# Two transformer layers with routed experts: the token table without weights, its one-hots on VectorE, output additions on GpSimd

## What is computed

```python
# layer 0: 8 experts of width 256, top 2, softmax router, shared width 1024
x = x + tanh(g_ffn[0]) * ffn0(layernorm(x))
# layer 1: 32 experts of width 192, top 6, sigmoid router, shared width 384
x = x + tanh(g_ffn[1]) * ffn1(layernorm(x))

def ffn(x):                                  # both, in outline
    topk_w, topk_i = top_k(score(x @ gate_w), K)
    topk_w = topk_w / sum(topk_w)
    combine = one_hot(topk_i) weighted by topk_w       # tokens x experts
    routed = einsum(silu(x @ wg[e]) * (x @ wu[e]) @ wd[e], combine)
    shared = silu(x @ sg) * (x @ su) @ sd
    return routed + shared
```

## Time and profile before

| | |
|---|---|
| runs | 2045.34 us median of 3 (2045.24 to 2046.21) |
| profiled execution | 2046.07 us, its span 2044.0 us |
| mean granted clock of TensorE | 0.969 |
| busy TensorE | 1886.2 us (92% of the span) |
| busy VectorE | 1348.0 us (66%) |
| busy ScalarE | 1145.5 us (56%) |
| busy GpSimd | 782.2 us (38%) |

### The profile page before, as it was taken

How to read it: one execution, slowest core, us unless ns; L and a number is a source line. 1 busy time by engine, 2 the same in 40 slices (tenths; PEclk the granted TensorE clock), 3 DMA queues, 4 the chain that set the end, 5 groups by cost and what they waited for, 6 DMA issues and landing times. The chain is left out here.

```text
span 2044.0 us, 40829 instructions
## 1 busy us (share of the span) xinstructions
PE 1886.2 (92%) x10024; PEld 1220.2 (60%) x10025; DVE 1348.0 (66%) x2556; ACT 1145.5 (56%) x1857; POOL 782.2 (38%) x941
## 2 busy tenths in 40 slices
PE   5999999989999999994999999987888999999998
PEld 2333333344888878872433333345667888888886
DVE  6899988841445544436889988859984555555553
ACT  1777777753322335541777777762224566666664
POOL 3222222125201125553222222127644656565555
PEclk9999999999999999995999999988999999999998
DMA  4422222142111458665422222131027888888886
GB/s 141 119 59 64 61 66 64 40 172 97 55 55 56 144 175 196 139 107 138 123 67 59 65 60 67 45 136 39 1 96 180 190 196 203 194 201 201 204 186 107
DMA packets 100082, 233.53 MB, mean 114 GB/s; under 512 B 17410, under 2 KB 20484, under 8 KB 99972
## 3 DMA queue, kind: packets, MB, share of 16 engines
q1 hardware_dynamic: 61572, 137.75, 23.7%
q0 software_dynamic: 33792, 79.71, 20.1%
q10 hardware_dynamic: 4608, 14.68, 2.2%
HBM read 127.23 MB, written 57.67 MB: 90 GB/s over the span
## 5 line engine op out<-in xcount | busy, mean ns | idle before, releaser
L599 DVE TENSOR_REDUCE maxima<-ring_ps 128x1 f32<-128x512 f32 x1024 | 639.8, 681 | 89.2 <-PE ring_ps L386 88.2
L493 ACT ACTIVATE probs<-score_ps 128x1024 f32<-128x1024 f32 x512 | 501.8, 1019 | 91.6 <-PE score_ps L403 89.3
L386 PE MATMUL ring_ps<-k_turned,q_turned 64*128 64x512 f32 x1024 | 414.3, 481 | 39.7 <-DMA q_turned<-q_lo 18.4
L386 PEld LDWEIGHTS ring_ps<-k_turned,q_turned 64*128 64x128 f32 x1024 | 179.0, 193 | 367.1 <-DVE maxima L599 258.0
L1179 PE MATMUL bank_f<-w_gu_parts_f,xg_T_f 128*128 x1800 | 367.1, 352 | 2.1 <-issue 2.1
L1179 PEld LDWEIGHTS bank_f<-w_gu_parts_f,xg_T_f 128*128 128x128 f32 x1800 | 325.8, 190 | 30.4 <-issue 3.0
L403 PE MATMUL score_ps<-q_turned,k_turned 64*128 64x512 f32 x1024 | 336.3, 447 | 1.7 <-ACT probs L493 1.4
L420 PE MATMUL out_ps<-probs,v_ones 128*32 128x512 f32 x2048 | 273.3, 606 | 10.7 <-issue 10.4
L1204 PE MATMUL bank_f<-w_dn_parts_f,hg_T_f 96*128 (+1 forms) x888 | 243.6, 410 | 1.5 <-DVE hg_T_f L1773 1.5
L983 POOL DMA_INDIRECT xg_f<-xh_rows_f,idx_in_f x156 | 159.5, 1022 | 186.1 <-DVE idx_in_f L1663 106.7
L999 POOL DMA_INDIRECT out_x<-y_tok_f,idx_out_f x111 | 177.2, 1596 | 133.0 <-ACT y_tok_f L1407 94.6
(11 more groups left out here) (232 smaller groups left out, 2335.2 us busy)
## 6 DMA issues: line engine op xcount, KB each, us to landing
w_gu_f<-in_L_w_gu SPq DMA_DIRECT2D x64, 384.0 KB
q_turned<-q_hi SPq DMA_DIRECT2D x128, 128.0 KB, 2.6
w_raw_f<-in_L_w_sh_gu ACTq DMA_DIRECT2D x28, 512.0 KB, 3.5
w_dn_f<-in_L_w_dn SPq DMA_DIRECT2D x32, 384.0 KB
k_turned<-k_hi SPq DMA_DIRECT2D x128, 64.0 KB, 2.1
q_turned<-no_max SPq DMA_DIRECT2D x64, 128.0 KB, 2.6
q_turned<-q_lo SPq DMA_DIRECT2D x64, 128.0 KB, 2.7
w_gu_f<-in_L_w_gu SPq DMA_DIRECT2D x16, 512.0 KB
```

What stands on the lines that cost most here:

```text
L386: pe.matmul(ring(k, "max", i), q_turned[rows, slot, h // 2, c * P:(c + 1) * P], k_turned[rows, slot, :], start=True, stop=True).then_inc(m ...
L493: act.activation(probs[:, (TPB * u + c) % PROBS, pair, :, :], score_ps[:, pair, :, :], ACT.Exp, scale=float(D) ** -0.5).then_inc(exped, 1)
L599: dve.tensor_reduce(maxima[:, par, col:col + 1], ring(k, "max", i), AX.X, ALU.max).then_inc(max_taken, 1)
```

## The change

1. **Table of tokens alone.** The tile one-hot is scaled by the token number only and has 128 columns, not 384; the table product has 128 columns. `entry`, `weights_of` and the evacuation of weights go.
2. **Weights gathered.** `xh_rows` has H + E columns: the weights of the token for every expert are stored behind its normalized row (one more DMA by SyncE, behind `weight_made`), and the gather brings both. In `x_hi`, ScalarE then reads the tile's expert number into a register and copies that expert's column of `xg` to `table_sb[:, i, 1]` (`weight_taken`). GpSimd's gather into the same half waits for it.
3. **One-hots.** VectorE makes the slot one-hot right before the tile one-hot, each as one `tensor_scalar`; GpSimd makes none.
4. **Outputs.** In the groups below SOFT_GROUPS (1 in layer 0, as before; 3 in layer 1) ScalarE reads the banks and GpSimd adds. SyncE's stores of these groups wait for `y0_added`.
5. **Row blocks side by side.** In the down products, blocks 0 and 1 are done together for each f, then 2 and 3 one after the other.
6. VectorE makes the splits of x and w for the next group ahead of the one-hots after a group; the one-hots at the end of the output loop go.

```diff
-    KS = min(K, 3)
+    SOFT_GROUPS = 1 if layer == 0 else B - 1
-        xh_rows = dram("xh_rows", (ROWS, H))
+        xh_rows = dram("xh_rows", (ROWS, H + E))
@@ SyncE
+            sp.wait_ge(weight_made, 1)
+            sp.dma_start(xh_rows[0:TOK, H:H + E].rearrange("(n p) e -> p n e", p=P), weight[:]).then_inc(weight_stored, 16)
...
-                sp.wait_ge(y_read, TPB * b + TPB)
+                if b < SOFT_GROUPS:
+                    sp.wait_ge(y0_added, TPB * b + TPB)
+                else:
+                    sp.wait_ge(y_read, TPB * b + TPB)
@@ GpSimd
-            pool.wait_ge(places_ready, 1)
-            for n in range(HOTS):
-                slot_one_hot(n)
-            for c in range(TPB):
-                add_y0(c)
-            for n in range(HOTS, PAIRS):
-                slot_one_hot(n)
+            for c in range(TPB * SOFT_GROUPS):
+                add_y0(c)
             pool.wait_ge(table_ready, 1)
+            pool.wait_ge(weight_stored, 16)
+            pool.wait_ge(y0_added, TPB * SOFT_GROUPS)
...
                 pool.wait_ge(xg_turned, i + 3)
+                pool.wait_ge(weight_taken, i + 3)
                 gather(i + 4, half)
@@ TensorE, table_sum
-                mm = pe.matmul(bank[:, TABLE_BANK, 0:3 * P], slot_hot[:, n % HOTS, :],
-                               tile_hot[:, n % HOTS, :, :].rearrange("p c t -> p (c t)"),
+                mm = pe.matmul(bank[:, TABLE_BANK, 0:P], slot_hot[:, n % HOTS, :],
+                               tile_hot[:, n % HOTS, :],
@@ TensorE, shared_group
+                if g > 0:
+                    pe.wait_ge(y_read, TPB * g)
+                for f in range(FC):
+                    pe.wait_ge(h_done, g * FC + f + 1)
+                    for c in range(2):
+                        down_part(c, f)
+                for c in range(2, TPB):
+                    pe.wait_ge(y_read, TPB * g + (c - 1))
+                    for f in range(FC):
+                        down_part(c, f)
@@ ScalarE
+            def outputs(g):
+                for c in range(TPB):
+                    act.wait_ge(y_done, TPB * g + c + 1)
+                    if g >= 1:
+                        act.wait_ge(y0_added, TPB * g + (c - 3))
+                    act.activation(y0(c), bank[:, 6 + c % 2, :], ACT.Copy, scale=gate[:, 0:1]).then_inc(y_read, 1)
...
                     shared_x_hi(g + 1)
                     shared_w_hi(n + 1)
+                    if g < SOFT_GROUPS:
+                        outputs(g)
@@ ScalarE, x_hi
                 act.activation(xg_T[:, half, 0, :, :].rearrange("p d m -> p (d m)"), bank[:, 6, :], ACT.Copy).then_inc(xg_hi, 1)
+                expert = act.value_load(sched[0:1, bass.ds(i, 1), 0:1].rearrange("a i c -> a (i c)"), min_val=0, max_val=E - 1)
+                act.activation(table_sb[:, bass.ds(i, 1), 1:2].rearrange("p a c -> p (a c)"),
+                               xg[:, half, bass.ds(expert + H, 1)], ACT.Copy).then_inc(weight_taken, 1)
@@ VectorE, tile_one_hot
-                dve.scalar_tensor_tensor(tile_hot[:, n % HOTS, :, :], count_f[:, None, :].to_broadcast([P, 3, P]),
-                                         tile_of[:, i, k:k + 1],
-                                         entry[:, i, k, :, None].bitcast(F32).to_broadcast([P, 3, P]),
-                                         ALU.is_equal, ALU.mult).then_inc(tile_hot_made, 1)
+                dve.tensor_scalar(slot_hot[:, n % HOTS, :], count_f[:], slot_of[:, i, k:k + 1], None, ALU.is_equal
+                                  ).then_inc(slot_hot_made, 1)
+                dve.tensor_scalar(tile_hot[:, n % HOTS, :], count_f[:], tile_of[:, i, k:k + 1], token_f[:, i:i + 1],
+                                  ALU.is_equal, ALU.mult).then_inc(tile_hot_made, 1)
@@ VectorE, main order
-            weights_of(0)
             shared_x_lo(1)
             shared_w_lo(FC, 0)
             shared_w_lo(FC, 1)
-            for k in range(KS, K, KS):
-                tile_one_hots(HOTS)
-                weights_of(k)
+            tile_one_hots(HOTS)
...
                 if g + 1 < B:
+                    shared_x_lo(g + 1)
+                    for o in range(2):
+                        shared_w_lo(n + 1, o)
                     tile_one_hots(used + HOTS)
-                    shared_x_lo(g + 1)
                 for c in range(TPB):
-                    if g + 1 < B and c < 2:
-                        shared_w_lo(n + 1, c)
-                    dve.wait_ge(y_done, TPB * g + c + 1)
-                    if c == 0:
-                        dve.wait_ge(y_read, TPB * g)
-                    xc = x[:, g * TPB + c, :]
-                    dve.scalar_tensor_tensor(xc, bank[:, 6 + c % 2, :], gate[:, 0:1], xc, ALU.mult, ALU.add).then_inc(y_read, 1)
+                    if g >= SOFT_GROUPS:
+                        dve.wait_ge(y_done, TPB * g + c + 1)
+                        if c == 0:
+                            dve.wait_ge(y_read, TPB * g)
+                        xc = x[:, g * TPB + c, :]
+                        dve.scalar_tensor_tensor(xc, bank[:, 6 + c % 2, :], gate[:, 0:1], xc, ALU.mult, ALU.add).then_inc(y_read, 1)
...
-                    if c + 1 == TPB and g + 1 < B:
-                        tile_one_hots(used + HOTS_AHEAD)
```

More of the change, by code:

```diff
@@ L764, in make_ffn @@
         sched_ready, sched_out, sched_in = sem("sched_ready"), sem("sched_out"), sem("sched_in")
[L765 to L766 removed]
+        slot_hot_made, tile_hot_made, hot_used = (sem(n) for n in
+            ("slot_hot_made", "tile_hot_made", "hot_used"))
         table_ready = sem("table_ready")
@@ L786, in y0 @@
         def y0(c):
-            return (y_tok if c < 2 else xg)[:, c % 2, :]
+            return (y_tok if c < 2 else xg)[:, c % 2, 0:H]
         def raw_w(n, o):
@@ L1344, in _ @@
             shared_w_hi(FC)
-            for c in range(TPB):
-                act.wait_ge(y_done, c + 1)
-                act.activation(y0(c), bank[:, 6 + c % 2, :], ACT.Copy, scale=gate[:, 0:1]).then_inc(y_read, 1)
+            def outputs(g):
[4 more added lines that the diff above has]
+                    act.activation(y0(c), bank[:, 6 + c % 2, :], ACT.Copy, scale=gate[:, 0:1]).then_inc(y_read, 1)
+            outputs(0)
             for n in range(FC, B * FC):
@@ L1521, in _ @@
             then(dve.tensor_scalar(stat2[:], stat2[:], gate[:, 0:1], None, ALU.mult))
-            then(dve.tensor_tensor(weight[:], prob[:], over_e(stat2), ALU.mult))
+            dve.tensor_tensor(weight[:], prob[:], over_e(stat2), ALU.mult).then_inc(weight_made, 1)
             dve.wait_ge(ranked, 1)
@@ L1680, in finish_table @@
                                               ALU.is_lt, ALU.mult))
[L1681 to L1684 removed]
+                dve.scalar_tensor_tensor(table_sb[:, 0:P, 0], bank[:, TABLE_BANK, 0:P], -1.0, part, ALU.add, ALU.add
+                                         ).then_inc(table_ready, 1)
                 dve.wait_ge(table_ready, 1)
```

63 lines of the change are left out of this document (18 added, 45 removed).

## The result

The changed kernel takes 2037.35 us, median of 20 runs (2029.76 to 2046.36); the kernel before, run beside it, 2046.13 us, median of 20. The ratio is 0.9964, 95% interval 0.9954 to 0.9974: 0.36% faster, about 7 to 9 us, where 19 were forecast. The profiled execution took 2034.74 us, its span 2032.9 us at a mean granted clock of 0.970.

The account below looks back on a forecast made before the run. TensorE was taken to bound layer 0's shared part and the expert loops, VectorE layer 1's shared part. Layer 0's -1.6 and layer 1's -17.5 made -19.1 from 2046.07: 2027.0, as median 2026.3, range 2010 to 2044.

Parts of the forecast that it names:

- layer 0's shared part: Layer 0 before its expert loop, TensorE full: -2.9 us from the narrower table product, +0.6 from row blocks side by side.
- The two loops together: Expert loops of both layers: +8 for later gathers in layer 1, +1.5 and +0.7 at the starts of the loops.
- The table product: TensorE's shared parts: 128 columns instead of 384 take 0.09 us against 0.18, -2.9 us in layer 0.
- Row blocks side by side: Down products: +0.6 us in layer 0 for waits on block 0's reading, -1.3 at the end of layer 1's group 3.
- One-hots on VectorE: Layer 1's shared part: tile and slot one-hot take 0.47 us a pair; group 1's gate and up end at 1429.6, -16.4 us.
- Groups 2 and 3: Layer 1's shared part: group 2 takes 34.7 us against 42.1, with 3 of collisions, -7.4; group 3 gains 2.
- Gathered weights: Expert loops: gathers wait for ScalarE's copy, start about 1 us later; +8 in layer 1's loop, +1.5 at its start.
- The view on DMA: Rival for layer 1's expert loop: gathers become the bound, 44 us in place of 8, 2062 in all; chance 0.11.
- The third rival: Layer 1's shared part: ScalarE, reading 8 more outputs, becomes late by some 9 us in groups 1 and 2; 2045, chance 0.07.

Follow-up runs that it names:

- the seven experiments: Seven follow-up kernels that keep the changed kernel's expert loop; layer 1's loop took 520.4 to 523.9 us, layer 0's 189.3 to 192.1.
- e13: e12 with the down products' row blocks one after the other again; 2025.30 us, ratio 0.9905 to the kernel before.
- e5: Changed kernel with 416 unused bytes behind zero_tile in layer 0 and 288 in layer 1, x_parts to w_sh_parts a multiple of 2048 bytes; 2032.99 us.
- e9: Changed kernel with the down products' row blocks one after the other again; 2036.68 us in one execution.
- e12: e5 with ScalarE's copy of the weight column moved to the start of a step, before silu; 2024.19 us, ratio 0.9897 to the kernel before.
- e14: e13 with the slot one-hots back on GpSimd and SOFT_GROUPS = 1 in layer 1; 2021.71 us, ratio 0.9884 to the kernel before.
- e3: Changed kernel with 32 unused bytes per partition behind zero_tile in both layers; 2037.16 us, ratio 0.9962 to the kernel before.
- e4: Changed kernel with 64 unused bytes per partition behind zero_tile in layer 0; 2038.65 us in one run.
- e6: Changed kernel without the weight column's copy, its register load and the wait for it, longer rows kept; 2033.24 us, 4.373 a tile in layer 1's loop.
- e7: e6 with the longer gathered rows dropped as well; 2032.85 us, 4.357 us a tile in layer 1's loop.
- e2: Kernel before with 32 unused bytes per partition behind zero_tile in layer 0; 2049.14 us in one run.
- e15: e13 with SOFT_GROUPS = 1 in layer 1, slot one-hots staying on VectorE; 2024.82 us, ratio 0.9904 to the kernel before.

## Why the prediction was right in sign and wrong in size

The sum was -19.1; the profiled execution came out 11.3 below the kernel before's, the medians 8.8 apart. The steps that failed are the sum's -2.3 for layer 0's shared part, which came out at +2.5, and its -7.4 and -2 for groups 2 and 3 of layer 1, which came out at -5.3 and +1.3. The first failed mostly by a term put at nothing, the change of the tensors' places. The two loops together were forecast at +10.2 and came out at +7 in the profiled execution and at +12 to +19 in the seven experiments. In terms:

- **The table product.** -2.9 us in layer 0 from 0.09 against 0.18. Measured: 281.7 before against 279.6 in e13, where placement and row blocks are as before: -2.1. The next product starts even earlier than forecast (0.057), but 0.053 of that is lost at the one after it, which shows as 0.58 for a step in layer 1: 0.06 is saved per table product, not 0.09.
- **Not in the sum at all: placement.** +3.1 us in layer 0 (284.2 against 281.1 in e5). The prediction costed what the diff does to instructions, and not that it moves w_sh_parts.
- **Row blocks side by side.** +0.6 in layer 0; measured 1.5 in e9 and 2.2 between e12 and e13, since the one wait costs a group 0.5 and not 0.2. The -1.3 in layer 1's last group was right in kind: 0.9 (8.99 against 9.91 us for the down products).
- **One-hots on VectorE.** 0.47 a pair; measured 0.45. Group 1's end at 1429.6; measured 1430.95, in a stage that began 1.9 later. This step was right as a forecast of the time, and right that VectorE's list had to get shorter. That the slot one-hots must be on VectorE for it was not: e14 has the same stage length without them.
- **Groups 2 and 3.** 34.7 us for group 2; measured 36.8. VectorE's list from its split of x to its last h part was 32.3 us instead of 30.9: the collisions with GpSimd's additions were 4.2 us and not 3 (two splits of w at 1.7 us instead of 0.6, the first pair of one-hots at 2.46 instead of 0.45), and there were four other operations, not three. TensorE then ended 0.5 later. TensorE's time at the lower clock level in that group (3.4 us) cost nothing visible, for it waited for one-hots again behind it. -2 for group 3; measured 38.8 against 37.5 before, +1.3. There the wait of 2.79 us was followed by 6.5 us at the lower level and by no other wait for one-hots, so the slower steps were lost time; no term held that. In e3, e4, e6 and e7, without such a stretch there, group 3 took 36.4 to 36.6. The kernel before had 6.8 us of the lower level in its group 3 too.
- **Gathered weights.** The gather starts about 1 us later: measured 2.6 against 1.57 after the transposes. +8 for the loop and +1.5 at its start; measured +8.9 in the profiled execution, +12 to +15 in the others. TensorE's waits for gathered rows were put at about 8 us in all; measured 7.3. Mechanism and place were right (e6, e12), the size somewhat small. The view on DMA, that longer rows might bind, was given 0.11 and did not come: 0.016 us a tile. The prediction's estimate by the Trainium skill ("DMA: Bandwidth & Descriptors", How a descriptor splits into AXI transactions) was some 9% more per gathered row; e6 against e7 shows under 2 us in the whole loop.
- **The third rival**, ScalarE late by 9 us in two groups: TensorE's waits for ScalarE's output were 1.04 and 1.03 us in the changed kernel, near the 1.5 of the forecast.

The range of 2010 to 2044 held the time. That is no merit of the sum: its upper end was made of gathers and collisions, and of the 10 us missing between the medians, 3 came from placement, which no part of the range stood for.

## What to carry to other kernels

Cost a moved wait by what stands ahead of it in the waiting engine's order: the same 0.2 us copy cost 9 to 15 us behind x_hi, 6 before it and about 1 at a point where ScalarE was idle. When a diff changes the size of a tensor, compare the start-to-start time of products that it doesn't touch before believing any other account. Undo each part of a change that has several: here the two moves to other engines carried none of the gain, the gathered weights cost 9 to 15 us only by where their copy stood, and row blocks side by side cost 1.5 us in layer 0 for 0.9 in layer 1. Read a difference of 2 us in a stage beside the clock that was granted in it before giving it to an edit.

## What the runs showed of the hardware that I had not expected

- The place of operands in memory sets the pace of products at the same clock: behind a table product of 384 columns, sixteen products of 512 columns took 3.66 us where w_sh_parts of layer 0 stood at 155552 and 3.72 to 3.73 in e2; behind one of 128 columns, 3.71 at 155552 (e5, e12 to e15) and 3.78 to 3.79 at the three other addresses tried. In layer 1, 24 such products took 5.50 to 5.66.
- Products whose row blocks alternate between two banks run at the pace of one block after the other, 0.227 us apart; one wait whose idle time the profile gives as 0.16 us made the 96 products 0.5 us longer.
- A product of 128 columns lets the next start after 0.06 us, but a step of it and two others is 0.58 us long, 0.12 more than two products of 0.23.
- Within one shape of the stage, TensorE's time at the lower clock level ranged from 6.8 to 16.9 us, and the stage from 140.0 to 143.4.
- Two tensor_scalar one-hots of 128 elements take 0.45 us together on VectorE, and 1.3 each beside additions of GpSimd.
